# One packed matmul for the rest chunk, expert units of 112-slot tiles, and the adjacency stored by groups

## The reference

```python
# x (10000, 128), adj (10000, 10000), all float32
def gnn(user, item, adj, W_item, b_item, W_user, b_user):
    h = item @ W_item.T + b_item
    b = user @ W_user.T + b_user
    return relu(adj @ h + b)

def ffn(h, gate_w, gate_b, w1, b1, w2, b2):          # E = 8, C = ceil(1.25 * T / E) = 1563
    probs = softmax(x @ gate_w + gate_b)
    idx = argmax(probs); prb = probs[idx]
    pos = rank of the token among those of its expert
    kept = pos < C
    buf[idx, pos] = x                                 # (E, C, 128), tokens past C are dropped
    hmid = relu(buf @ w1 + b1)                        # (E, C, 512)
    ybuf = hmid @ w2 + b2                             # (E, C, 128)
    y = ybuf[idx, min(pos, C - 1)] * (prb * kept)
    return nan_to_num(y, nan=0.0, posinf=10000.0, neginf=-10000.0)

x = x + gnn(layernorm(x), item_feat, adj, ...)
x = x + ffn(layernorm(x), ...)
```

## Time and profile before

| | us |
|---|---|
| median of 3 runs | 1457.16 (1450.68 to 1458.88) |
| the profiled execution | 1441.39 |
| its span | 1439.6 |
| graph stage, to PE's last matmul of the last block | 0 to about 1187 |
| routing of the last blocks, clears and scatters | to about 1227 |
| expert stage | to 1439.6 |

### The profile page before, as it was taken

The page is one execution under the profiler, slowest core; times in us unless marked ns, Lnnn a source line. Parts: engine busy times, 40 slices in busy tenths (PEclk is TensorE's granted clock), DMA queues, the critical chain, the costliest instruction groups (busy, mean ns, idle before and its releaser), DMA issues. The chain is left out here.

```text
span 1439.6 us, 20443 instructions
## 1 busy us (share of the span) xinstructions
PE 1365.8 (95%) x6318; PEld 1108.8 (77%) x6318; DVE 1167.7 (81%) x1714; ACT 983.8 (68%) x1010; POOL 565.1 (39%) x426
## 2 busy tenths in 40 slices
PE   7999999999999999999999999999999991899992
PEld 6878888888888888888888888888888871678771
DVE  7897978879879798798797987987979862388774
ACT  5686776767667767776677667766777650788870
POOL 0001235053151350532514405225144176288887
PEclk9999999999999999999999999999999995899996
DMA  8999999999999999999999999999999933323220
GB/s 331 354 416 409 362 361 352 355 354 353 360 352 355 353 353 355 353 357 354 359 351 353 355 352 358 350 362 345 362 352 362 347 118 101 91 76 93 72 67 3
DMA packets 88369, 434.31 MB, mean 302 GB/s; under 512 B 22526, under 2 KB 24070, under 8 KB 88328
## 3 DMA queue, kind: packets, MB, share of 16 engines
q1 hardware_dynamic: 67296, 416.42, 79.0%
q0 software_dynamic: 17952, 12.25, 3.2%
q10 hardware_dynamic: 3080, 5.12, 1.0%
HBM read 421.51 MB, written 23.50 MB: 309 GB/s over the span
## 5 line engine op out<-in xcount | busy, mean ns | idle before, releaser
L591 DVE TENSOR_TENSOR a_lo<-raw,a_hi 128x2000 fp32r<-128x2000 f32 (+1 forms) x400 | 863.3, 2188 | 145.1 <-ACT a_hi L427 141.3
L427 ACT CAST a_hi<-raw 128x2000 fp32r<-128x2000 f32 (+1 forms) x400 | 722.6, 1825 | 189.5 <-PE bank L939 164.3
L937 PE MATMUL bank<-a_hi,h_hi 128*128 128x500 f32 (+1 forms) x1580 | 636.1, 403 | 0.9 <-ACT a_hi L427 0.8
L939 PE MATMUL bank<-a_hi,h_lo 128*128 128x500 f32 (+1 forms) x1580 | 614.5, 389 | 0.0
L949 PE MATMUL bank<-a_lo,h_hi 128*128 128x500 f32 (+1 forms) x1580 | 428.5, 391 | 0.0
L937 PEld LDWEIGHTS bank<-a_hi,h_hi 128*128 128x128 f32 (+1 forms) x1580 | 297.4, 188 | 72.8 <-issue 17.9
L949 PEld LDWEIGHTS bank<-a_lo,h_hi 128*128 128x128 f32 (+1 forms) x1580 | 295.2, 188 | 71.8 <-issue 13.7
L939 PEld LDWEIGHTS bank<-a_hi,h_lo 128*128 128x128 f32 (+1 forms) x1580 | 298.3, 189 | 59.1 <-issue 4.4
L828 POOL TENSOR_TENSOR late<-ve,neghalf 125x4 f32<-125x4 f32 x20 | 22.4, 1121 | 666.4 <-DVE ve L608 666.4
L836 POOL DMA_INDIRECT records<-late,slot x80 | 194.3, 2429 | 22.9 <-issue 22.6
L902 POOL DMA_INDIRECT out<-raw,toki x128 | 134.4, 1050 | 35.7 <-issue 34.2
(11 more groups left out here) (114 smaller groups left out, 940.4 us busy)
## 6 DMA issues: line engine op xcount, KB each, us to landing
raw<-adj_m SPq DMA_DIRECT2D x380, 1000.0 KB, 5.3
raw<-adj_m SPq DMA_DIRECT2D x20, 500.0 KB
raw<-records SPq DMA_DIRECT2D x32, 202.1 KB
late<-items_t SPq DMA_DIRECT2D x19, 256.0 KB, 4.7
xb<-x ACTq DMA_DIRECT2D x20, 224.0 KB
raw<-w SPq DMA_DIRECT2D x8, 258.5 KB, 3.6
raw<-w SPq DMA_DIRECT2D x8, 256.0 KB, 2.9
out<-raw,toki POOLq DMA_INDIRECT x128
```

Of the source, the lines that this page charges most:

```text
L427: last = nc.scalar.copy(a_hi[:, g % HI_RING, 0:m], raw[:, g % RAW, 0:m])
L591: last = v.tensor_tensor(a_lo[:, g % RAW, 0:m], raw[:, g % RAW, 0:m], a_hi[:, g % HI_RING, 0:m].bitcast(F32), ALU.subtract)
L937: nc.tensor.matmul(acc[q][:, 0:BLOCK], h_hi[0:m, k * HID:(k + 1) * HID], a, start=(k == 0), stop=False)
L939: last = nc.tensor.matmul(acc[q][:, 0:BLOCK], h_lo[0:m, k * HID:(k + 1) * HID], a, start=False, stop=False)
```

## The change

Three things are changed at once.

1. *The rest chunk is packed.* `adj_r` is stored three times under one another, 48 rows (`PACK`). ACT casts 48 rows to `a_hi`; DVE then overwrites rows 32 to 47 of `a_hi` with the difference. In h_hi the rest chunk's rows 16 to 31 get h_lo and rows 32 to 47 get h_hi again, by two DMAs that SP issues once, in block 1 after the load of group 2 (`pack_h`). One matmul of 48 rows, at the end of the low part of the last group, replaces the three. Since it reads `a_hi` of ring place 3, ACT's cast of group 3 of the next block gets a wait on `lo_used`.
2. *Expert units of 112-slot tiles.* An expert's 1568 slots are 14 tiles of 112 in units of 4, 3, 4 and 3 tiles: 448 or 336 columns. `toki` is gone, since the record holds the token number as an integer that the indirect DMA reads itself; for this the zero strip gets NO_TOKEN in 14 places by a second memset. `yout` has four buffers. The output's lag is 4, and on PE the output transposes stand behind the first products. `load_rec` waits on `sent` of its buffer's last unit where it waited on `toki_ready`.
3. *Adjacency in DRAM by groups*, each a 128 x 2048 array with rows at a pitch of 8192 bytes, of which 8000 are read; before, a row of a group began 156,000 bytes behind the one above.

```diff
-SLOT_P = 98
-UNIT = 4 * SLOT_P
+SLOT_P = 112
+UNIT_TILES = (4, 3, 4, 3)
-LAG_IN, LAG_MID, LAG_Y, LAG_OUT = 1, 2, 3, 5
+LAG_IN, LAG_MID, LAG_Y, LAG_OUT = 1, 2, 3, 4
...
-                    sp.dma_start(raw[:, g % RAW, 0:n], adj_b[:, a:a + n],
+                    sp.dma_start(raw[:, g % RAW, 0:n], adj_g[:, 0:n],
                                  max_dma_last_dim=16384).then_inc(raw_loaded[g % RAW], 16)
+                    if fixed and b == 1 and g == 2:
+                        pack_h()
                     if last:
-                        sp.dma_start(raw[0:REM, g % RAW, n:n + BLOCK], rem_b).then_inc(raw_loaded[g % RAW], 16)
+                        sp.dma_start(raw[0:PACK, g % RAW, n:n + BLOCK], rem_b).then_inc(raw_loaded[g % RAW], 16)
...
+            def pack_h():
+
+                sp.wait_ge(h_lo_ready, GROUPS)
+                cols = slice(FULL * HID, CHUNKS * HID)
+                sp.dma_start(h_hi[REM:2 * REM, cols].bitcast(F32), h_lo[0:REM, cols].bitcast(F32)).then_inc(h_packed, 16)
+                sp.dma_start(h_hi[2 * REM:PACK, cols].bitcast(F32), h_hi[0:REM, cols].bitcast(F32)).then_inc(h_packed, 16)
...
+                if g == HI_RING - 1 and (not isinstance(b, int) or b > 0):
+                    act.wait_ge(lo_used, b * GROUPS)
...
-                    last = v.tensor_tensor(a_lo[0:REM, g % RAW, m:n], raw[0:REM, g % RAW, m:n],
-                                           a_hi[0:REM, g % HI_RING, m:n].bitcast(F32), ALU.subtract)
+                    last = v.tensor_tensor(a_hi[2 * REM:PACK, g % HI_RING, m:n], raw[2 * REM:PACK, g % RAW, m:n],
+                                           a_hi[2 * REM:PACK, g % HI_RING, m:n].bitcast(F32), ALU.subtract)
...
+                if g == GROUPS - 1:
+                    if isinstance(b, int) and b == 0:
+                        pe.wait_ge(h_packed, 32)
+                    c = FULL - FIRST[g]
+                    last = nc.tensor.matmul(acc[q][:, 0:BLOCK], h_hi[0:PACK, FULL * HID:CHUNKS * HID],
+                                            a_hi[0:PACK, g % HI_RING, c * BLOCK:(c + 1) * BLOCK],
+                                            start=False, stop=True)
...
                 if wait:
-                    sp.wait_ge(toki_ready, q - BODY + 1)
-                    sp.wait_ge(yout_ready, q - BODY + 1)
+                    sp.wait_ge(yout_ready, taken)
+                    sp.wait_ge(sent[k % UNITS_E], landed)
...
+                p.memset(zeros[0:TP, :].rearrange("p (r c) -> p r c", c=REC)[:, :, C_TOK:C_TOK + 1].bitcast(U32),
+                         NO_TOKEN).then_inc(zeros_set, 1)
+                pool.wait_ge(zeros_set, 2)
...
-                    wait_on_pool(pool, recq_loaded[r], (i + (k - LAG_OUT + 1) // BODY + 1) * 16, 2)
-                    p.tensor_scalar(toki[:, r, :].unsqueeze(2), recq[:, r, :, C_TOK:C_TOK + 1],
-                                    float(NO_TOKEN), None, ALU.add).then_inc(toki_ready, 1)
...
+            for n in range(UNITS):
+                pool.wait_ge(yout_ready, n + 1)
+                for j in range(tiles(n)):
+                    p.indirect_dma_start(out, bass.IndirectOffsetOnAxis(
+                        ap=recq[:, n % BODY, j, C_TOK:C_TOK + 1].bitcast(U32), axis=0),
+                        yout[:, n % UNITS_E, j, :], None, bounds_check=USERS - 1,
+                        oob_is_err=False).then_inc(sent[n % UNITS_E], 16)
```

More of the change, by code:

```diff
@@ L23 @@
 REM = ITEMS - FULL * 128
+PACK = 3 * REM
 CHUNKS = FULL + 1
@@ L28 @@
 GMAX = max(SIZES)
+GROUP_PITCH = 2048
 RAW = 10
@@ L40 @@
 CAP = -(-5 * USERS // (4 * EXPERTS))
-SLOT_P = 98
-UNIT = 4 * SLOT_P
-UNITS_E = -(-CAP // UNIT)
-SLOTS_E = UNITS_E * UNIT
+SLOT_P = 112
+UNIT_TILES = (4, 3, 4, 3)
+UNITS_E = len(UNIT_TILES)
+UNIT_AT = [sum(UNIT_TILES[:k]) * SLOT_P for k in range(UNITS_E)]
+UNIT = max(UNIT_TILES) * SLOT_P
+SLOTS_E = sum(UNIT_TILES) * SLOT_P
+assert SLOTS_E >= CAP and UNIT <= 512
 SLOTS = EXPERTS * SLOTS_E
@@ L529, in step @@
                         act.wait_ge(x2q_turned, s - 1)
-                    for j in range(4):
+                    for j in range(tiles(k)):
                         last = nc.scalar.activation(x2q[:, k % 2, j, :], recq[:, k, j, 0:HID], ACT.Identity,
@@ L1047, in step @@
                         pe.wait_ge(x2q_lo_ready, s - 1)
-                    for j in range(4):
+                    for j in range(tiles(k - LAG_IN)):
                         last = nc.tensor.transpose(ps_in[:, j * SLOT_P:(j + 1) * SLOT_P],
```

153 lines of the change are left out of this document (75 added, 78 removed).

## The result

In the first comparison the changed kernel took **1443.23 us** (median of 7 runs, 1441.45 to 1446.91) and the kernel before 1451.49 us (7 runs, 1450.68 to 1458.88): a ratio of **0.9931**, 95% interval 0.9909 to 0.9952. It is faster, by 0.7%. Forecast were 1424 us and a range of 1409 to 1438: the sign was right, and the time lies above the range.

What follows compares the result with a forecast made beforehand. PE was taken to pace the graph stage and POOL's chain the end of the expert stage. Terms -14.8 - 19.2 + 1.0 = -33.0 us, taken from the 1457.2 us median, gave 1424 us, range 1409 to 1438.

Steps and rivals of the forecast that it cites:

- the base: Whole run: the 15.8 us between profiled execution (1441.4) and median (1457.2) is carried over unchanged to the new kernel.
- Rest chunk: End of each graph-stage block on PE: two short matmuls go, 0.74 us in each of 20 blocks, -14.8 us (-12.8 to -16.8).
- ACT's wait: Graph stage: ACT's delayed cast of group 3 costs nothing, since 3.6 us of lead over PE are left.
- Packing h: Block 1, once: SP stops until h_lo is there, delaying later loads; cost 0 to 1.5 us, taken as 0.
- Pitch: Graph-stage loads: the new adjacency layout changes nothing, as PE does not wait for loads; 0 us.
- rival D: Graph-stage loads become the bound because equal power-of-two rows collide in DRAM: about 1625 us, chance 0.05.
- the clearing: POOL between the stages: a second memset and a wait before the clears, +1.0 us (0.3 to 1.5).
- Rival C: Last block: POOL's indirect DMA of 9.56 us shrinks to 1.33, later work starts 8.2 us earlier: 1416 or 1409 us, chance 0.12.
- Expert stage: PE at 5.45 us a unit, POOL's debt gone, span ending 1.6 us after the last DMA: -19.2 us (-13 to -22).
- Rival B: Expert stage: weights arrive late behind SP's new wait and ACT stalls, 9 us: 1433 us, chance 0.14.
- Rival E: Timed runs' extra 16 us is PE waiting for loads, hiding the rest chunk's gain: 1439 us, chance 0.07.
- Rival F: PE waits at each block's start for the delayed cast, 1 us x 19: 1443 us, chance 0.02.

Runs made afterwards that it cites:

- quiet: Kind of comparison in which the kernel before takes about 1442 us; the changed kernel, unedited, took 1420.14 and 1420.71 us there.
- second comparison: The changed kernel timed again with no edit, beside the kernel before: 1420.14 us against 1442.78, ratio 0.9847.
- disturbed: Kind of comparison in which everything takes longer: kernel before 1451.49 and 1463.20 us, changed kernel, unedited, 1443.23 and 1444.95 us.

## Why the prediction was wrong, point by point

Against the trace of before (span 1439.58) I set the quiet one of the second comparison (1417.82), 21.8 us less; forecast were 33.0. Of the 11.2 us between, POOL's end, carried over at 1.6 us and 9.8 in fact, is 8.2; what lies between the stages, 3.8 and not 1.0, is 2.8; the expert stage up to its last DMA is 2.3; and the graph stage gave 2.0 more than forecast. The other step that failed is the base, the 15.8 us added for both kernels alike.

**Rest chunk, -14.8 forecast: right in kind, a little low.** At a block's end the starts of the changed kernel, first comparison, answer to the earlier trace rows; the last row answers to the earlier trace rows:

```profile
880.39 1.06 PE L966 MATMUL bank<-a_lo,h_hi 128*128 128x500 f32 x4
881.29 0.93 PE L1012 MATMUL bank<-cst,colsT 128*125 128x8 f32 x8
...
883.76 0.39 PE L957 MATMUL bank<-a_hi,h_lo 128*128 128x500 f32 x1
883.99 0.61 PE L966 MATMUL bank<-a_lo,h_hi 128*128 128x500 f32 x2
884.53 0.49 PE L973 MATMUL bank<-a_hi,h_hi 48*128 48x500 f32 x1
884.96 0.49 PE L955 MATMUL bank<-a_hi,h_hi 128*128 128x500 f32 x1
...
885.14 3.64 ACT L449 CAST a_hi<-raw 128x2000 fp32r<-128x2000 f32 x2 [2.33 <-PE bank L973]
```

The full high part is followed by the low part after 0.23 us, as forecast. Blocks went from 57.94 to 57.10, 0.84 us each and not 0.74, inside the bounds. The sum missed 0.1 us behind the short pair. The rows of before for the low part's end:

```profile
895.02 0.94 PE L988 MATMUL bank<-cst,colsT 128*125 128x8 f32 x8
...
898.26 0.49 PE L949 MATMUL bank<-a_lo,h_hi 16*128 16x500 f32 x1
898.68 0.49 PE L937 MATMUL bank<-a_hi,h_hi 128*128 128x500 f32 x1
```

The four low matmuls behind the pair took 894.01 to 895.02, 1.01 us, and take 0.90 now, since the first of them stood 0.33 us ahead of the next start and not 0.23: that is the 0.1 us which the sum left out. And the 16-row matmul took 0.42 us to the next start where the one of 48 rows takes 0.43, so its price was unchanged, as forecast. The last block gave 3.5. ACT's copy of the graph product of the last block comes 16.8 us earlier in the quiet trace and 17.9 in the first; the quiet one was 1.1 us later from its first blocks on.

**ACT's wait, 0: right.** The cast of group 3 waits for the packed matmul and ends at 887.0; PE begins that group at 890.48, so 3.5 us of lead were left, 3.6 forecast.

**Packing h, 0: right.** SP, ACT and PE, first block to second, answer to the earlier trace rows:

```profile
81.28 0.59 SPq L369 DMA_DIRECT2D h_hi<-h_lo  x1
81.92 0.58 SPq L370 DMA_DIRECT2D h_hi<-h_hi  x1
82.55 6.82 SPq L355 DMA_DIRECT2D raw<-adj_m  x8
...
85.61 0.50 PE L973 MATMUL bank<-a_hi,h_hi 48*128 48x500 f32 x1
...
87.44 1.87 ACT L449 CAST a_hi<-raw 128x2000 fp32r<-128x2000 f32 x1 [1.07 <-DMA raw<-adj_m]
```

PE takes the packed weights without a wait between its neighbours.

**Pitch, 0: right,** by the run with the old layout; rival D is out. The Trainium skill, page DMA: Bandwidth & Descriptors, section "Latency and other measured facts", has copies lose rate at row pitches of 2 MiB and more, and 512 KiB at 207 GB/s beside 214 with a padded pitch. These runs agree that 8 KiB loses none: blocks last 57.10 us with either layout.

**Between the stages, 0 forecast beside the clearing: a loss of 3.8 us, a rival's mechanism turned round.** Of the graph stage's 16.8 us only 13.0 are left when the first record is normalized. POOL's rows of the last block, first comparison, answer to the earlier trace rows:

```profile
1148.59 9.49 POOL L863 DMA_INDIRECT records<-late,slot  x1 [0.30 <-issue]
...
1166.27 1.19 POOL L867 DMA_INDIRECT out<-late,kept_out  x1 [0.30 <-issue]
1167.45 1.66 POOL L874 MEMSET h_raw<- 125x1848 f32 x1
1169.17 0.12 POOL L876 MEMSET h_raw<- 125x14 uint32 x1
1170.12 0.96 POOL L884 DMA_INDIRECT records<-h_raw,clear_edge  x1 [0.83 <-POOL h_raw L876]
...
1188.55 0.20 POOL L331 TENSOR_TENSOR carrier_pool<-ones 125x1 f32<-125x1 f32 x1 [6.42 <-issue]
```

Rival C had the DMA of 9.56 us vanish with the shifted timing. It did not: 9.49 us, in the same run of four subtractions of DVE. But it is now the second of the block's eight DMAs and was the fourth, so two more of 1.5 us are left to do after it, and all that follows on POOL comes 3 us later; the clearing adds 0.2, and 0.6 I can't place.

**The clearing, +1.0: too high.** From the first memset's start to the first clear it is 2.67 us now and was 2.50: +0.2. The small memset takes 0.12; the wait of 0.83 moved behind it, and I had counted it twice.

**Expert stage, -19.2: two of its parts right, one term missing.** In the quiet trace DVE's last output came 14.8 us earlier within the stage and POOL's last DMA another 2.1 us, 16.9 in all. POOL's debt went as forecast: it waits for DVE in 14 places, 31.0 us.

```profile
POOL out L923 <- DVE raw L837: 31.0, 14, 2.7
```

PE's step is 5.51 us and not 5.45: 31 x 0.06 = 1.9 us of the 2.3 missing. Rival B's 9 us did not come; ACT waits for four of the weights, 0.8 us at most, and the run with a lag of 5 showed the cliff behind it. The missing term is the end: +8.2 us (9.78 less 1.61). I had carried over 1.6 us, "the span 1.6 us later", from tiles of 98 rows. It was a constant of the old form, and no row of before shows the new one. I bounded the DMA's price for 112 rows from both sides (before's own rows had it: the clears of the earlier trace rows are DMAs of 112 rows, 0.96 us) and not what comes after it.

The terms: -16.8 for the graph stage, +3.8 between the stages, -16.9 and +8.2 in the expert stage: -21.7 of 21.8 measured.

**The base.** I took 15.8 us between the profiled execution and the median over, as something that both kernels would pay alike. In quiet comparisons it isn't there: before takes 1442. In the disturbed first one it is 10 us for before, by its 7 runs, and 23 us for the changed kernel. So this step failed too: the changed kernel's time lies 23.6 us above what the terms give from the profiled execution (1419.6), not 15.8. From the forecast to the measured time: 11.2 us of terms, -5.7 since before's median fell from 1457.2 to 1451.5 with more runs, and 13.5 that the disturbance takes from the changed kernel beyond what it takes from before; 1424.2 + 19.0 = 1443.2. Put by steps, the terms failed by 11.2 us, of which POOL's end alone is 8.2, and the base by 7.8. Rival E named the same 16 us and had them in the graph stage, as waits for loads. In the changed kernel they are in the expert stage, as late news of PE's work; the graph stage doesn't show them. Rival F named 1443 us, the measured number, by luck: it had PE wait at each block's start, and PE doesn't. What makes a comparison disturbed stays open. That the quiet time, 1420 us, lies near 1424 is chance: a base too high by 15 hid terms too good by 11.

## What to carry to other kernels

Ask of a difference between a profiled execution and the timed ones where it would sit, before it is carried over: here the stage with short hand-overs between four engines paid for it and the one paced by TensorE alone did not, and the two kernels paid unequally. When two measurements of one kernel differ by more than the effect, measure the unchanged kernel again beside its parent before explaining a stall; it cost one run here and threw out three theories. And if the form of an instruction changes, the constant behind the last one of it is unknown too.

## What the runs showed of the hardware

- In the disturbed traces PE's semaphore updates came up to 4 us late while it went on starting matmuls, and then seven within 0.4 us. The starts of matmuls in a profile don't show it; a wait of its reader on "remote", and missing records, do. The Trainium skill, page Perfetto Trace Analysis, section "Tensor Engine Instruction (MATMUL, LD_WEIGHTS)", has the update pushed when PSUM has acknowledged the write, after the estimated end that a profile shows; the quiet trace agrees with a push after the start by a nearly fixed time, 0.46 to 0.55 us for a unit's last product; in the disturbed one it was 2.0 us for the one at 1253.17. The Trainium skill, page NOTIFIC — the notification-queue block, section "7.1 Overflow: three behaviours, one of which stalls the engine", knows record rings that drop records when full and an inner path that can hold up engines; missing records and late updates together would fit, but no run here shows that it is the cause.
- An indirect DMA of POOL at its shortest takes 0.96 us with 98 rows, 0.94 with 112, 1.11 to 1.13 with 114 and 1.19 with 125, each followed by 0.30. Beside DVE's subtractions one took 9.5 us.
- After a stream of such DMAs of 112 rows the program ends 9.8 us after the last, POOL being the last engine; with 98 rows 1.6 to 1.9 us, with 114 2.6.
- Among full matmuls of 500 columns, 0.227 us apart, a single short one takes 0.42 us (16 rows) or 0.43 (48 rows) to the next start, and the start ahead of it and the one behind it are 0.31 to 0.33 apart from their successors.
